# Expert tiles prepared four ahead in four banks, a gather gated by gate-and-up, and keys and queries without the class token

## The reference

```python
out = jnp.concatenate([cls, proj], axis=1) + pos_embed           # (64, 37, 256)
sim = einsum('bid,bjd->bij', q, k) * scale                       # 16 heads of 64
sim = sim + cope(q, sim, pos_emb)                                # a position term from the scores
h = layernorm(h + (softmax(sim) @ v) @ Wout + b_out)
# the feed-forward part: a router takes the 2 best of 8 experts for each token
y = einsum('enf,efh->enh', silu(g) * u, down_w)                  # g, u: gate and up, 256 wide
h = layernorm(h + shared(h) + routed(y))                         # shared: a dense part of 512
```

## Time and profile before

| | |
|---|---|
| median of 3 runs | 759.18 us (758.54 to 761.34) |
| the profiled execution | 758.44 us, its span 756.7 us |
| PE busy | 722.8 us, 96% of the span |
| VectorE, ScalarE, GpSimd busy | 524.3, 387.9, 122.4 us |
| mean granted TensorE clock | 0.993 |
| attention | from the start to about 480 us |
| expert tiles | from 550 to 697 us |

### The profile page before, as it was taken

The page is one execution under the profiler, slowest core; times in us unless marked ns, Lnnn a source line. Parts: engine busy times, 40 slices in busy tenths (PEclk is TensorE's granted clock), DMA queues, the critical chain, the costliest instruction groups (busy, mean ns, idle before and its releaser), DMA issues. The chain is left out here.

```text
span 756.7 us, 14650 instructions
## 1 busy us (share of the span) xinstructions
PE 722.8 (96%) x5106; PEld 624.0 (82%) x5107; DVE 524.3 (69%) x1094; ACT 387.9 (51%) x752; POOL 122.4 (16%) x162
## 2 busy tenths in 40 slices
PE   7999999999999999999999998999899888999994
PEld 5887897979798897979798886687788788898883
DVE  3377988989898888989898899797822222222664
ACT  1556557474646557474646555522155444453463
POOL 2000000000000000000000000100046566664131
PEclk9999999999999999999999999999999999999998
DMA  9951010010101010010000016100022222220811
GB/s 279 301 172 36 1 53 20 25 47 24 47 24 47 0 44 27 24 35 24 12 24 13 1 48 199 47 11 1 1 66 71 69 70 75 66 67 33 271 65 51
DMA packets 27532, 47.11 MB, mean 62 GB/s; under 512 B 3626, under 2 KB 18768, under 8 KB 27500
## 3 DMA queue, kind: packets, MB, share of 16 engines
q1 hardware_dynamic: 23072, 36.91, 15.3%
q0 software_dynamic: 4224, 9.71, 4.0%
q10 hardware_dynamic: 204, 0.07, 0.1%
HBM read 35.40 MB, written 13.12 MB: 64 GB/s over the span
## 5 line engine op out<-in xcount | busy, mean ns | idle before, releaser
L1260 PE MATMUL ps_S<-attnT,v_sb 128*128 128x128 f32 x704 | 88.2, 279 | 10.8 <-ACT attnT L1567 10.7
L1260 PEld LDWEIGHTS ps_S<-attnT,v_sb 128*128 128x128 f32 x704 | 83.2, 194 | 13.4 <-ACT attnT L1567 13.1
L701 POOL TENSOR_TENSOR rs<-ve,neg_half 111x2 f32<-111x2 f32 x11 | 12.2, 1110 | 457.9 <-DVE ve L1808 457.9
L2143 DVE COPY attnT<-ps_S 128x256 f32<-128x256 f32 x44 | 18.6, 424 | 97.2 <-PE ps_S L1274 52.6
L1716 DVE COPY_PREDICATED table<-bit,table 111x112 f32<-111x112 int16 (+6 forms) x110 | 75.1, 683 | 11.2
L872 PE MATMUL ps_X<-wkv_sb,hT 128*111 128x512 f32 (+1 forms) x176 | 80.5, 598 | 0.0
L916 PE MATMUL ps_X<-oT,wout_sb 128*128 128x222 f32 x320 | 61.9, 351 | 0.0
L916 PEld LDWEIGHTS ps_X<-oT,wout_sb 128*128 128x128 f32 x320 | 60.1, 190 | 0.2 <-issue 0.2
L797 PE MATMUL ps_S<-hT,wq_sb 128*128 128x222 f32 (+1 forms) x320 | 60.0, 345 | 0.0
L872 PEld LDWEIGHTS ps_X<-wkv_sb,hT 128*111 128x111 f32 (+1 forms) x176 | 28.5, 173 | 35.5 <-issue 34.5
L797 PEld LDWEIGHTS ps_S<-hT,wq_sb 128*128 128x128 f32 x320 | 57.6, 189 | 0.1
(11 more groups left out here) (301 smaller groups left out, 1386.3 us busy)
## 6 DMA issues: line engine op xcount, KB each, us to landing
down_sb<-in_x_dram SPq DMA_DIRECT2D x10, 648.0 KB
gu_sb<-y_d SPq DMA_DIRECT2D x8, 512.0 KB, 6.6
h_d<-hT SPq DMA_DIRECT2D x11, 222.0 KB, 2.5
kept<-h_d SPq DMA_DIRECT2D x11, 222.0 KB, 2.6
h_d<-h SPq DMA_DIRECT2D x10, 222.0 KB
wkv_sb<-in_L_attn_Wkv_dram SPq DMA_DIRECT2D x2, 1024.0 KB, 12.4
gu_sb<-in_L_ffn_gate_w_dram SPq DMA_DIRECT2D x2, 1024.0 KB, 10.9
gu_sb<-in_L_ffn_up_w_dram SPq DMA_DIRECT2D x2, 1024.0 KB, 11.7
```

What stands on the lines that cost most here:

```text
L1260: mm = nc.tensor.matmul(S[:, i, j * FF + f * P:j * FF + f * P + P], held[:, i, k, j, f * P:f * P + P], xgT[:, i, k], start=(k == 0), stop= ...
```

## The change

Three edits.

**Tiles four ahead.** The expert tiles get four PSUM banks `S[:, 0..3]` for gate and up, four places of `xgT` (now in `oT`), of `held` (two in `v_sb`, two in `wout_sb`) and of the SiLU result `thg` (two in `gate`, two in `u`). PE turns the rows of t+4 in tile t, does gate and up of t+2 ahead of the wait for `hid` of t, and then the down product of t. ACT copies the weights and rows of t+4. Weights of t+4 wait for gate and up of t. The first copies into `wout_sb` and `oT` wait until the tile lists have been made, which read them.

**A gate for the gathers.** In POOL's loop, gather t+6 now also waits for `tile_gu` of t+2.

**Queries and keys without the class token.** `by_pair` multiplies the 216 columns of patches, `hT[:, k, :n, 1:]`, which are six runs of 36 with a gap of one between them, into 216 contiguous columns of the bank. The copies to `qT` and `kT` skip the class token's columns, which keep the values that pair 0 wrote.

```diff
             for t in range(NT):
                 if t + 6 < NT:
+                    pool.wait_ge(tile_gu, t + 3)
                     gather_next(t + 6, (t + 2) % 4)
                 scatter_y(t, t % 4)
...
-                        mm = nc.tensor.matmul(bank[:, i * COLS:i * COLS + n * TOK], w[:, k, c:c + P],
-                                              hT[:, k, :n], start=(k == 0), stop=(k == KE - 1))
+                        mm = nc.tensor.matmul(bank[:, i * NPAT:i * NPAT + n * (TOK - 1)], w[:, k, c:c + P],
+                                              hT[:, k, :n, 1:], start=(k == 0), stop=(k == KE - 1))
...
             def transpose_x(t, turn, b):
                 pe.wait_ge(tile_x[b], turn * 16 + 16)
+                if not isinstance(t, int) or t >= 2:
+                    pe.wait_ge(tile_xt_sb, t - 1)
...
                 t, i = turn * 4 + b, b % 2
-                if ahead >= 3:
-                    transpose_x(t + 3, turn + (b + 3) // 4, (b + 3) % 4)
+                if ahead >= 4:
+                    transpose_x(t + 4, turn + 1, b)
+                if ahead >= 2:
+                    gate_up_tile(t + 2, (b + 2) % 4)
                 pe.wait_ge(tile_hid, t + 1)
-                if ahead >= 2:
-                    gate_up_tile(t + 2, i)
...
-            def hold(t, i, e):
+            def hold(t, b, e):
 
-                if not isinstance(t, int) or t >= 2:
-                    act.wait_ge(tile_gu, t - 1)
+                if not isinstance(t, int) or t >= 4:
+                    act.wait_ge(tile_gu, t - 3)
...
-            def tile(t, i, ahead, e_ahead):
-                if ahead >= 3:
-                    hold(t + 3, 1 - i, e_ahead)
-                    x_in_sbuf(t + 3, 1 - i)
+            def tile(t, b, ahead, e_ahead):
+                if ahead >= 4:
+                    hold(t + 4, b, e_ahead)
+                    x_in_sbuf(t + 4, b)
                 if ahead >= 2:
-                    tanh_tile(t + 2, i)
+                    tanh_tile(t + 2, (b + 2) % 4)
```

More of the change, by code:

```diff
@@ L53, in vit_tower @@
     NT = (TOPK * REAL - NEXP) // P + NEXP
-    AT_ONCE = 7
-    NTX = NT + AT_ONCE - 4
+    AT_ONCE = 4
+    NTX = NT
     assert NT % 4 == 0 and NEXP == 8 and G % 2 == 0 and G2 > 4
@@ L428, in embedded, with of_patches @@
             return X[:, 0, m * NPAT:(m + 1) * NPAT]
+        def of_patches(bank):
+            return bank[:, :2 * NPAT].rearrange("p (f b t) -> p f b t", f=2, b=2 * TPG)
         def of_group(bank):
@@ L1259, in gate_up_tile @@
                         for k in range(KE):
-                            mm = nc.tensor.matmul(S[:, i, j * FF + f * P:j * FF + f * P + P],
-                                                  held[:, i, k, j, f * P:f * P + P], xgT[:, i, k],
+                            mm = nc.tensor.matmul(S[:, b, j * FF + f * P:j * FF + f * P + P],
+                                                  w[:, k, j, f * P:f * P + P], xgT[:, b, k],
                                                   start=(k == 0), stop=(k == KE - 1))
@@ L1291, in _ @@
                 for b in range(4):
-                    tile(four, b, 3, of[b])
+                    tile(four, b, 4, of[b])
             of = experts(NT // 4 - 1)
             for b in range(4):
-                tile(NT // 4 - 1, b, min(3, 3 - b), of[b])
+                tile(NT // 4 - 1, b, 3 - b, of[b])
             pe.wait_ge(tile_hid, NT)
@@ L1563, in _, with x_in_sbuf, tanh_tile @@
                     shared_tanh(c, f)
-            def x_in_sbuf(t, i):
+            def x_in_sbuf(t, b):
                 act.wait_ge(tile_xt, t + 1)
-                nc.scalar.copy(xgT[:, i], X[:, i, :EMB].rearrange("p (k r) -> p k r", k=KE)
+                nc.scalar.copy(xgT[:, b], X[:, b % 2, :EMB].rearrange("p (k r) -> p k r", k=KE)
                                ).then_inc(tile_xt_sb, 1)
-            def tanh_tile(t, i):
+            def tanh_tile(t, b):
                 act.wait_ge(tile_gu, t + 1)
-                nc.scalar.activation(thg[:, i], S[:, i, :FF], ACT.Silu).then_inc(tile_tanh, 1)
+                nc.scalar.activation(thg[b], S[:, b, :FF], ACT.Silu).then_inc(tile_tanh, 1)
             def experts(four):
@@ L1603, in _ @@
                 x_in_sbuf(t, t)
-            hold(2, 0, of[2])
+            act.wait_ge(lists_t, 1)
+            hold(2, 2, of[2])
             tanh_tile(0, 0)
-            x_in_sbuf(2, 0)
+            x_in_sbuf(2, 2)
+            hold(3, 3, of[3])
             tanh_tile(1, 1)
+            x_in_sbuf(3, 3)
             with act.Fori(0, NT // 4 - 1) as four:
-                of = experts(four)
+                of = experts(four + 1)
                 for b in range(4):
-                    tile(four * 4 + b, b % 2, 3, of[b + 3])
-            of = experts(NT // 4 - 1)
+                    tile(four * 4 + b, b, 4, of[b])
             for b in range(4):
-                t = NT - 4 + b
-                tile(t, t % 2, min(3, NT - 1 - t), of[b + 3])
+                tile(NT - 4 + b, b, 3 - b, None)
             def spread(half):
@@ L2133, in _, with hidden_tile @@
             shared_sum(NEW)
-            def hidden_tile(t, i):
+            def hidden_tile(t, b):
                 dve.wait_ge(tile_tanh, t + 1)
-                V.tensor_tensor(hid[:, i], thg[:, i], S[:, i, FF:], ALU.mult).then_inc(tile_hid, 1)
+                V.tensor_tensor(hid[:, b % 2], thg[b], S[:, b, FF:], ALU.mult).then_inc(tile_hid, 1)
             def y_tile(t, turn, b):
@@ L2150, in _ @@
                 for b in range(4):
-                    hidden_tile(four * 4 + b + 1, (b + 1) % 2)
+                    hidden_tile(four * 4 + b + 1, (b + 1) % 4)
                     y_tile(four * 4 + b, four, b)
```

29 lines of the change are left out of this document (15 added, 14 removed).

## The result

| | before | after |
|---|---|---|
| median | 758.86 us (758.37 to 761.34, 4 runs) | 753.13 us (752.52 to 753.28, 4 runs) |
| ratio to before | 1 | 0.9919 (95% interval 0.9906 to 0.9932) |
| profiled execution, span | 758.4, 756.7 us | 753.05, 751.3 us |
| first to last down product | 135.7 us | 134.1 us |

The change gained 5.7 us where 13.3 were forecast. The page shows TensorE as busy a share of the span as before, and a new entry in the chain of work that ended last, the gather, where before's gave most to TensorE.

What follows compares the result with a forecast made beforehand. TensorE was taken as the bound: its own work in attention, 16.3 us of pauses from late signals in the expert tiles. 758.4 - 11.2 - 2.1 = 745.1, plus 0.7 for the median: 745.9 us; range 740 to 764.

Steps and rivals of the forecast that it cites:

- dense indirect DMAs hold TensorE's signals back: Expert tiles: GpSimd's indirect DMAs issued one behind another make TensorE's signals 3.8 us late, behind 16.3 us of pauses.
- tiles four ahead hide the old pauses: Expert tiles: the deeper order hides 5.0 us of signal lateness, so all 16.3 us of pauses could go.
- slack 0.1: Gated gather in the expert tiles: landing taken as 2.6 us, leaving 0.1 us before its rows are needed.
- L: Lateness of the gate and up signal that opens a gather, taken as about 0.35 us, mean of four cases.
- 2.87 + (L - 0.1)/2: Time of an expert tile behind the gate: 2.995 us, giving back 5.1 of 16.3 us.
- rival (b): Expert tiles: L near 0.9 costs 0.4 us a tile, only the queries' 2 us left: 757 us; chance 0.18.
- The gate itself makes such gaps: GpSimd's queue in the expert tiles: a late signal holds the next gather back, and GpSimd falls silent.
- -2.1: Queries and keys in attention: 576 matmuls over 216 columns instead of 222, 3.6 ns less each, -2.1 us.
- the bound of -2.9: Queries and keys in attention: best case, 5 ns less for each of 576 matmuls, -2.9 us.
- 1.4 ns: Queries and keys: cost per matmul of breaks between runs of 36 columns, from the patches' runs of six.
- -11.2: Expert tiles: gain from 16.3 us of pauses removed, less 5.1 us given back by the gated gather.

Runs made afterwards that it cites:

- e13: e4 with gathers as plain DMAs of fixed rows on SyncE's queue, GpSimd only scattering, output not computed: 736.0 us where the kernel before takes 761.2.
- e14: e4 with two TensorE signals a tile in place of three, VectorE's copy waiting for the next transposes: 750.11 us, ratio 0.9855.
- e15: e4 without the wait for gate and up ahead of a gather: 753.51 us, ratio 0.9901.
- sets 2 and 3: Two comparisons of four runs each, kernels with seven gathers ahead and variants, then before and after again; the kernel before took 743.0 us in both.
- e6: e4 with scatters replaced by SyncE stores in tile order, GpSimd only gathering, output not computed: stage 119.6 us.
- e1: The changed kernel without the gate for the gathers: 758.12 us.
- e4: The changed kernel with gathers one tile further ahead, seven before the loop, behind the same gate: 750.0 us, ratio 0.9862.
- e10: The changed kernel run again, nothing altered, in a set with signals on time: 744.94 us, ratio 1.0026 to the kernel before.
- e11: The same kernel as e4, seven gathers ahead, run again in a set with signals on time: 740.65 us.
- e2: The kernel before with only the gate for the gathers added: 755.89 us.

## Why the prediction was wrong

**Right in part: where the pauses come from, in a set like the first.** "I take it that dense indirect DMAs hold TensorE's signals back": that GpSimd's indirect DMAs have a part in it is shown by e13, 0.01 us late, beside e14 and e15 of the same set, 3.8 and 5.2. What the prediction couldn't know is that this isn't always so: in sets 2 and 3 the same instructions hold nothing. That it is their density is not shown. The first five gathers of the kernel before, in a comparison with late signals, start 1.30 to 1.60 us apart, as close as later ones, and one signal that falls among them isn't held: a turning ends at 550.29 and its signal is on record at 550.30.

```profile
549.88 0.41 PE L1242 MATMUL ps_X<-ident,attn 128*128 128x128 f32 x2 [0.33 <-DMA attn<-h_d,ids_x]
```

Shown is that one scatter a tile on GpSimd isn't enough, and that its gathers are needed. Whether by the number of DMAs, by gathers and scatters taking turns, or because they are gathers of scattered rows was not told apart in such a set: e13 also reads rows that lie in order and by another queue, and e6, with gathers alone, ran in set 2.

**Right: tiles four ahead hide the old pauses.** No stop before gate and up by ACT's row copy is left in after. That alone proves little, since its signals are at most 1.3 us late and the old order hid 2.1; but none is left in e1 and e4 either, where they are 2.6 and 3.8 us late. It covers waits for data alone, though: the stops of TensorE itself, in e4, were not in the prediction.

**Wrong: "I take 2.6, nearer to the rows of the stage itself: slack 0.1".** This is the step that failed. The gather takes 2.83 and 2.93 us from GpSimd's start to the turning in the two rounds above (most others of after where TensorE waits for it have 2.83 to 2.94, two have 2.6), and the turning 0.27 to the gate and up, not 0.22. The sum, 5.74 - 0.27 - 1.95 - 0.84 - 2.93, is -0.25: there is no slack, and every round pays. e10 measures this term without any late signal: 4.5 us in the stage, where the prediction had nothing. e11 confirms it, since one tile more of lead brings the stage from 124.3 to 119.6 in the same set. The error was to read the landing from the window in which data moved, and not from the gather to the engine that waits for it; 3.07 in the chain was the nearer row. An estimate by the Trainium skill (DMA: Bandwidth & Descriptors, Anatomy of one DMA) has 2.3 us for these bytes. The trace does not agree, with 2.78 in the chain of after, and the measurement decides.

**Wrong: "For L I take the mean", and the formula 2.87 + (L - 0.1)/2.** The mean lateness in after is 0.28, even less than the 0.35 taken. But TensorE serves two chains of gathers, and one late chain sets the pace of both: in the round above the signal that opens the gather is 0.61 late and the other 0.03, and two tiles take 6.49. Worked out again: 6.02 and about 0.6 are 6.6, 0.44 a tile over 2.87, with which some 38 tiles lose 16 to 17 us; the trace has 134.1 - 119.6 = 14.5. The rival (b), "L near 0.9 costs 0.4 a tile", came near with its price and its 757 us, but not with its reason: L is 0.6 in every second tile, and the missing slack makes up the rest.

**Half right: "The gate itself makes such gaps".** Lateness fell from 1.04 to 0.28 us in the mean. But the gate alone (e2) leaves 0.95, and the gate with gathers that have a lead (e4) 1.22. What goes with the better signals of after is GpSimd's idle time of some 1.5 us in every round, which is there because the round trip is too long. So the gain in lateness seems to be paid for with the pauses themselves: in e4, where the lead removes them, GpSimd is dense again and the signals are late again. That one is the cause of the other was not tried by itself.

**Queries and keys, mis-sized.** -3.1 us where -2.1 was taken: breaks in runs of 36 columns cost nothing, and the bound of -2.9 was reached. The working that took 1.4 ns for them from the patches' runs of six doesn't carry over.

**The sum.** Forecast -11.2 and -2.1; measured -1.6 in the stage and -3.1. The two profiles have 0.7 us more ahead of the first down product, for which there is no term, and nothing behind the last (59.8 us in both). The range of 740 to 764 held the time.

## What to carry to other kernels

A wait added to break up an engine's bursts must have its whole round trip counted, from signal to turned rows, against the distance that the order leaves; if the slack is within 0.3 us of nothing, give the transfer another tile of lead at the same time. Where two chains share an engine, the later one sets the pace, so take the lateness of the worse chain, never the mean. And run the kernel before again beside each experiment: its own time moved by 2.4% from set to set here, and the change was a gain of 0.8% in one kind of set and a loss of 0.3% in the other.

## What the runs showed of the hardware

- TensorE's signals to ACT, DVE and GpSimd are held up to 3.8 us (5.2 in e15, without the gate) while GpSimd issues two indirect DMAs of 128 rows a tile, a gather and a scatter, 0.31 us apart; with one scatter a tile (e13) they are 0.01 us late. This holds in three comparisons (before 758.9, 760.8 and 761.2 us) and in none of the kernels of two others (before 743.0). Before, after and e4 ran there too, with the same instructions, and at the same gaps until the first signal is late. What differs from set to set is open. A late set and one on time both carry chip number 1, so if the number always means the same chip, the chip alone doesn't decide it. The granted clock was 0.99 or more in all.
- While signals are held, TensorE itself can stop in the middle of a group of matmuls without a wait (3.08 us from 606.45 in e4, in place of 1.95). Why was not settled; sparing a third of the program's signals changes nothing.
- A GpSimd gather of 128 rows of 1 KB takes 2.83 us (after) and 2.93 us (e10) from the start of its instruction to the first use of its rows in the rounds shown, and 0.83 and 0.84 more from the signal that opens it.
